# Another weave of the delta rule's streams, and the low parts of the first attention's queries and keys through a diagonal matmul

## The reference

```python
# first attention: 16 heads of width 8 (h=16, d=8), gated weights
qkv = jnp.einsum('bnk,ok->bno', x, g_qkv * qkv_weight)
dots = jnp.einsum('bhid,bhjd->bhij', q, k) * scale
out = jnp.einsum('bhij,bhjd->bhid', jax.nn.softmax(dots, axis=-1), v)
...
# delta rule: 16 heads of width 64, one state W per sequence and head
def step(W, inp):
    q_t, k_t, v_t, b_t = inp
    err = v_t - jnp.einsum('bhij,bhj->bhi', W, k_t)
    W_new = W + b_t[..., None, None] * jnp.einsum('bhi,bhj->bhij', err, k_t)
    return (W_new, jnp.einsum('bhij,bhj->bhi', W_new, q_t))
```

## Time and profile before

| | |
|---|---|
| median of 3 runs | 1710.97 us |
| the profiled execution: its time, its span | 1703.88 us, 1702.1 us |
| busy: PE, DVE, ACT, POOL | 1498.6, 1211.1, 909.4, 694.8 us |
| first attention | about 15 to 250 us of the span |
| the delta rule's 16 units | about 1098 to 1572 us |
| mean granted TensorE clock | 0.961 of full speed |

### The profile page before, as it was taken

One profiled execution on the slowest core, in us unless ns is written; L12 is line 12 of the kernel. 1 busy time (PEld: TensorE's weight loads), 2 busy tenths in 40 slices (PEclk: granted clock), 3 DMA queues, 4 the chain that ended last, 5 costly groups with the idle time before them and its releaser, 6 DMA issues.

```text
span 1702.1 us, 42055 instructions
## 1 busy us (share of the span) xinstructions
PE 1498.6 (88%) x18200; PEld 809.8 (48%) x18200; DVE 1211.1 (71%) x2245; ACT 909.4 (53%) x1269; POOL 694.8 (41%) x732
## 2 busy tenths in 40 slices
PE   7888878999999999999988877889888888989995
PEld 4222223333334334333424544777777777765452
DVE  7788877988857785867527668576777665574866
ACT  1676675777756675786582333545445543342210
POOL 1111131566555564665580107448675556000000
PEclk9898999999999999999999999989999999989898
DMA  4000003332222231432302000000000001100000
GB/s 155 1 1 1 1 1 112 100 88 80 82 72 72 73 102 44 115 85 72 88 1 79 1 1 13 15 15 16 4 16 16 16 4 45 43 3 1 7 7 13
DMA packets 32409, 70.66 MB, mean 42 GB/s; under 512 B 5328, under 2 KB 7056, under 8 KB 31968
## 3 DMA queue, kind: packets, MB, share of 16 engines
q1 hardware_dynamic: 32224, 67.98, 13.6%
HBM read 47.45 MB, written 20.51 MB: 40 GB/s over the span
## 4 chain that ended last, share of the span: by engine, by line
PE 55%; DVE 28%; ACT 8%; issue 6%; POOL 3%; DMA 0%; SPq 0%; ACTq 0%; DVEq 0%; POOLq 0%
PE ps L159 52%; DVE a_MX L408 5%; DVE b_mx L864 2%; ACT b_X L924 1%; POOL d_XI L1744 1%; PE ps L227 1%; POOL d_tmp L1741 1%; DVE st L171 1%; ACT d_L L168 1%; PE ps L1555 1%; DVE b_rd L1034 1%; DVE sq L206 1%; DVE b_VL L799 1%; DVE d_XE L1678 1%; DVE d_KV L1632 1%
## 5 line engine op out<-in xcount | busy, mean ns | idle before, releaser
L942 POOL TENSOR_TENSOR b_EL<-b_X,b_EH 128x1024 f16<-128x1024 f32 x160 | 341.2, 2133 | 235.6 <-ACT b_EH L168 235.6
L924 ACT ACTIVATE b_X<-ps 128x1024 f32<-128x1024 f32 x160 | 163.6, 1022 | 119.0 <-PE ps L159 117.6
L1741 POOL TENSOR_TENSOR d_tmp<-d_G,d_XI 128x31 f32<-128x31 f32 (+15 forms) x248 | 127.8, 515 | 184.3 <-DVE d_G L1670 165.5
L864 DVE TENSOR_REDUCE b_mx<-ps 128x2 f32<-128x1024 f32 x128 | 156.0, 1219 | 50.3 <-PE ps L159 48.6
L168 ACT ACTIVATE b_EH<-b_X 128x1024 f16<-128x1024 f32 x160 | 169.1, 1057 | 34.4 <-PE ps L159 23.2
L159 PE MATMUL ps<-b_M,b_S 128*128 128x512 f16 (+1 forms) x768 | 178.3, 386 | 2.4 <-ACT b_X L924 2.4
L408 DVE TENSOR_REDUCE a_MX<-ps 128x2 f16<-128x1024 f32 x128 | 155.2, 1225 | 27.4 <-PE ps L159 26.1
L445 ACT ACTIVATE a_E<-ps 128x1024 f32<-128x1024 f32 x128 | 131.1, 1024 | 76.1 <-PE ps L159 75.5
L1744 POOL TENSOR_TENSOR d_XI<-d_XI,d_tmp 128x31 f32<-128x31 f32 (+15 forms) x248 | 142.0, 573 | 19.4
L427 POOL TENSOR_TENSOR a_QS<-a_QS,a_MR 128x512 f16<-128x512 f16 x16 | 18.5, 1155 | 215.8 <-ACT a_MR L168 211.8
L159 PEld LDWEIGHTS ps<-b_M,b_S 128*128 128x128 f16 (+1 forms) x768 | 55.5, 98 | 101.4 <-issue 40.8
(11 more groups left out here) (324 smaller groups left out, 3430.9 us busy)
## 6 DMA issues: line engine op xcount, KB each, us to landing
b_S<-s_xk SPq DMA_DIRECT2D x48, 336.0 KB, 6.4
b_M<-s_xq SPq DMA_DIRECT2D x48, 256.0 KB, 5.1
s_xk<-b_Hk SPq DMA_DIRECT2D x16, 336.0 KB, 2.2
s_xk<-b_Lk SPq DMA_DIRECT2D x16, 336.0 KB, 2.4
s_xq<-b_Hq SPq DMA_DIRECT2D x16, 256.0 KB, 2.0
s_xq<-b_Lq SPq DMA_DIRECT2D x16, 256.0 KB, 2.0
d_XI<-eye SPq DMA_DIRECT2D x8, 512.0 KB, 3.7
f_w<-f_w SPq DMA_DIRECT2D x1, 2048.0 KB, 8.5
```

The source lines that it names most:

```text
L864: last = v.e.tensor_reduce(b_mx[:, 0, :, n], PS[:, bk:bk + 2, :], AX, ALU.max)
L924: a.e.activation(b_X[k % 2], PS[:, bk:bk + 2, :], ACT.Exp, scale=0.125).then_inc(sem("b_ex"), 1)
L942: last = p.e.tensor_tensor(b_EL[k % 6], b_X[k % 2], b_EH[k % 6], ALU.subtract)
L1741: e.tensor_tensor(tm, a, x, ALU.mult).then_inc(*p.step())
```

## The change

**First attention.** Two diagonal matrices a_dg (fp16, identity times the constant of queries and of keys) are made once on DVE. The product of a_HI with the constant is no longer made by DVE at the store: PE adds it to AUX with one 128x128x512 fp16 matmul (`a_lower_tensor`, start=False, in slots 1 and 3), and ACT then copies AUX to a_QS or a_KS (`a_store_scalar`, slots 1 and 3). `a_project_vector` is gone. ACT's rounding no longer waits on the store's semaphore, since PE's order covers it.

**Delta rule.** Only the order of instructions changes, by other numbers in the weave and a start value for two streams. The solves and all other matmuls are the same instructions as before. The weight 35 in `c_order` equals the old expression.

```diff
+        a_dg = rA.take("a_dg", 128, F16).rearrange("p (k n) -> p k n", k=2)
...
+            for k in range(2):
+                e.tensor_scalar(a_dg[:, k], ident16[:], a_cst[:, k:k + 1], None, ALU.mult).then_inc(sem("id16"), 1)
...
+        def a_lower_tensor(t, G, k):
+
+            t.wait_ge("id16", 3)
+            t.wait_ge("a_hi", 2 * G + k + 1)
+            mm(t.e, PS[:, AUX, :], a_dg[:, k], a_HI[k], start=False).then_inc(sem("a_qk"), 1)
...
-        def a_project_vector(v, G, k):
-            out = (a_QS, a_KS)[k][G % 4]
-            v.wait_ge("ld_cst", 16)
-            v.wait_ge("a_hi", 2 * G + k + 1)
-            v.wait_ge("a_sc", 8 * (G - 3))
-            stt(v.e, out, a_HI[k], a_cst[:, k:k + 1], PS[:, AUX, :], ALU.mult, ALU.add).then_inc(sem("a_st"), 1)
+        def a_store_scalar(a, G, k):
+            a.wait_ge("a_qk", 4 * G + 2 * k + 2)
+            a.wait_ge("a_sc", 8 * (G - 3))
+            copy(a.e, (a_QS, a_KS)[k][G % 4], PS[:, AUX, :]).then_inc(sem("a_st"), 1)
...
+                    if s in (1, 3) and p + 1 < NG:
+                        a_lower_tensor(t, p + 1, s // 2)
...
+        PREP_LEAD = {"dve": 0.25, "act": -0.25, "pe": 0.25}
+        ROWS_LEAD = {"pe": 0.5, "act": 0.25}
...
-                streams = [(chain(lane, u), 9)]
+                streams = [(chain(lane, u), 8.62)]
...
-                    streams.append((prep(lane, u + 1), 17))
+                    streams.append((prep(lane, u + 1), 17.34, -PREP_LEAD.get(lane.name, 0)))
...
-                    streams.append((rows(lane, m + 1), D_ROWS))
+                    streams.append((rows(lane, m + 1), 18.34, -ROWS_LEAD.get(lane.name, 0)))
...
-                    streams.append((later(13, turn(lane, m)), 30))
-                    streams.append((later(16, blocks(lane, m)), 24))
+                    streams.append((later(18, turn(lane, m)), 30.59))
+                    streams.append((later(22, blocks(lane, m)), 24))
```

More of the change, by code:

```diff
@@ L24 @@
 SHARED = {
-    "e_km": ("a_qk", 32), "e_kp": ("a_hi", 32), "e_vm": ("a_st", 32), "e_vp": ("a_vp", 4), "e_qm": ("a_v", 4),
+    "e_km": ("a_qk", 64), "e_kp": ("a_hi", 32), "e_vm": ("a_st", 32), "e_vp": ("a_vp", 4), "e_qm": ("a_v", 4),
     "e_q": ("a_mt", 128), "e_sm": ("a_mx", 128), "e_ms": ("a_mg", 16), "e_ng": ("a_mrow", 16), "e_mk": ("a_q2", 16),
@@ L35, in weave @@
 def weave(*streams):
-    live = [[g, n, 0] for g, n in streams]
+    live = [[x[0], x[1], x[2] if len(x) > 2 else 0] for x in streams]
     while live:
@@ L264, in build @@
         a_rec = rA.take("a_rec", 32)
+        a_dg = rA.take("a_dg", 128, F16).rearrange("p (k n) -> p k n", k=2)
+        assert rA.word <= 32160, rA.word
         rA = Room(nc, 38944)
@@ L299, in a_load_vector @@
             e.tensor_copy(ident16[:], ident[:]).then_inc(sem("id16"), 1)
+            v.wait_ge("ld_cst", 16)
+            v.wait_ge("id16", 1)
+            for k in range(2):
+                e.tensor_scalar(a_dg[:, k], ident16[:], a_cst[:, k:k + 1], None, ALU.mult).then_inc(sem("id16"), 1)
         def a_load_out_vector(v):
@@ L340, in a_split_gpsimd @@
                 p.wait_ge(f"ld_xt{b}", 16)
-                p.wait_ge("a_qk", 8 * (b - 1) if b > 2 else 0)
+                p.wait_ge("a_qk", 16 * (b - 1) - 1 if b > 2 else 0)
             e.tensor_copy(x[:, 0], w).then_inc(*p.step())
@@ L527, in a_tensor @@
                 hold(t, ACC, (16, 8)[k])
+                a_lower_tensor(t, 0, k)
             keys = b_keys_tensor(t, 0)
@@ L562, in a_scalar @@
                 a_project_scalar(a, 0, k)
+                a_store_scalar(a, 0, k)
             side = a_side(a, a_out_scalar, b_keys_scalar)
@@ L572, in a_scalar @@
                         a_project_scalar(a, p + 1, s // 2)
+                    if s in (1, 3) and p + 1 < NG:
+                        a_store_scalar(a, p + 1, s // 2)
                     if s == 4 and 0 < p <= NG:
@@ L585, in a_vector @@
             keys = b_keys_vector(v, 0)
-            for k in range(2):
-                a_project_vector(v, 0, k)
             side = a_side(v, a_out_vector, b_keys_vector)
@@ L597, in a_vector @@
                         a_den_vector(v, G - 1)
-                    if s in (1, 3) and p + 1 < NG:
-                        a_project_vector(v, p + 1, s // 2)
                     if p in (1, 2):
@@ L1403, in c_order @@
             second = experts(lane, 1)
-            weave((tail, B_OUT + 10), (both(experts(lane, 0, begun), part(second, 4)), 13))
+            weave((tail, 35), (both(experts(lane, 0, begun), part(second, 4)), 13))
             first = both(parts(lane, 0), both(rows(lane, 0), later(7, both(turn(lane, 0), blocks(lane)))))
@@ L2063, in d_order @@
                 m = u // 2 + 2
-                streams = [(chain(lane, u), 9)]
+                streams = [(chain(lane, u), 8.62)]
                 if u == 0:
-                    streams.append((keys(lane, 2), D_KEYS))
+                    streams.append((keys(lane, 2), 26.29))
                 if u == 1:
-                    streams.append((later(1, blocks(lane, 2)), 24))
+                    streams.append((later(0, blocks(lane, 2)), 24))
                 if u % 2 == 0 and u < 14:
-                    streams.append((later(20, back(lane, u // 2 + 1)), 24))
+                    streams.append((later(21, back(lane, u // 2 + 1)), 24))
                 if u + 1 < 16:
-                    streams.append((prep(lane, u + 1), 17))
+                    streams.append((prep(lane, u + 1), 17.34, -PREP_LEAD.get(lane.name, 0)))
                 if u % 2 and m + 1 < NH:
-                    streams.append((rows(lane, m + 1), D_ROWS))
+                    streams.append((rows(lane, m + 1), 18.34, -ROWS_LEAD.get(lane.name, 0)))
                 if u % 2 == 0 and 2 < m < NH:
-                    streams.append((later(13, turn(lane, m)), 30))
-                    streams.append((later(16, blocks(lane, m)), 24))
+                    streams.append((later(18, turn(lane, m)), 30.59))
+                    streams.append((later(22, blocks(lane, m)), 24))
                 if u in (2, 6):
@@ L2080, in d_order @@
                 if u in D_LATE:
-                    streams.append((late(lane, D_LATE[u]), 14))
+                    streams.append((late(lane, D_LATE[u]), 14.48))
                 if u > 12:
```

3 lines of the change are left out of this document (1 added, 2 removed).

## The result

The changed kernel takes 1668.6 us (median of 4 runs) against 1711.22 for the kernel before: ratio 0.9763, 95% interval 0.9729 to 0.9798. A second comparison, with six and seventeen runs, gave 1672.25 against 1707.57, ratio 0.9807 (0.9764 to 0.9849); one of the seventeen, 1909.62 us at a granted clock of 0.734, is left out of that ratio. So it is faster by 33 to 41 us, where I forecast 14.7.

What follows compares the result with a forecast made beforehand. PE, busy 88% of the time, was taken as the bound, so order could win only where it waits. Attention -1.7 and delta rule -13 made -14.7 us, taking the median 1710.97 to 1696; range 1683 to 1711.

Steps and rivals of the forecast that it cites:

- d_AT: Delta rule, two units: PE's wait of 1.75 us for this tile goes to zero, mean gain 1.7 us.
- d_OT: Delta rule, two units: outputs come ahead of the projection, so PE's wait for ACT's copy shrinks; 1.5 us gained.
- the chain: Delta rule: of PE's chain waits, 2.0 us a pair of units, half is taken as gained, -1.0 us.
- The wait for d_KT: Delta rule, two units: a new wait, as the gram matrix needs copies of key turns standing in a row; +0.85 us.
- that for the fold: Delta rule, odd units: a new wait, as the fold comes sooner behind the corner while ACT copies more keys; +0.5 us.
- POOL's wait for d_G: Delta rule: POOL's inverse waits 15.24 us for d_G; 12 or more would be left, so it stays hidden.
- A plain group: First attention, groups without layer norm: plus 0.5 us each (12.94 to 13.47), seven counted, +3.7 us.
- the terms -3.9 and +1.0: First attention: six stores among DVE-bound layer-norm pieces save 0.65 us each; four among small pieces cost 0.25 each.
- its rival's +8: First attention: costs +8 us if all 15 groups pay 0.5 and none gains, total 1706; no chance of its own.
- The rule on the clock: Attention group at 158.81: the page's rule lets shorter waits give back 1.5 us; the forecast said DVE sets the length, nothing gained.
- trade waits: Rival, delta rule: PE leaves one wait and meets the next, giving 0 to -5 us, about 1707; chance 0.20.
- The lump of transposes: Rival, delta rule: four DVE transposes together hold the values' scaling, a pair loses 2.1 us, total 1720; chance 0.10.

Runs made afterwards that it cites:

- mix: The changed kernel with the old weights and no leads in the weaves of units 1 to 11: 1670.1 us, ratio 0.9781.
- attention_only: The kernel before with the first attention's part of the change alone, the delta rule in its old order: 1699.8 us, ratio 0.9953.
- before_plus32: The kernel before with 32 more clock-holding matmuls at the program's start, equal columns: 1705.0 us, ratio 0.9984.
- after_again: The changed kernel, nothing altered, measured a second time against the kernel before: 1672.3 us, ratio 0.9807.
- delta_plus32: The kernel before with the delta rule's new order alone and 32 more clock-holding matmuls at the program's start: 1671.9 us, ratio 0.9790.
- after_less32: The changed kernel with 32 fewer clock-holding matmuls at the program's start, equal columns: 1688.3 us, ratio 0.9891.
- delta_order: The kernel before with the delta rule's new order alone, the first attention as it was: 1691.4 us, ratio 0.9902.
- ends_plus32: The kernel before with 32 more start matmuls and the new weights and leads only in units 0 and 12 to 15: 1702.4 us, ratio 0.9970.
- delta_shifts: The kernel before with only the later turns, blocks and back transposes and the turn's new weight: 1689.4 us, ratio 0.9898.
- the four positions: The changed kernel with 32 fewer, 0, 32 more and 64 more matmuls at the program's start: 1688.3, 1672.3, 1668.7 and 1678.4 us.

## Why the prediction was right or wrong

**The removed waits: right in the main. The bound: not.** Per pair (the list's 280 or 260 us hold 5.2 pairs) d_AT gave 0.8 where I took 1.7 (0.6 us a time are left, where I said none), d_OT 1.1 where I took 1.5, and the chain 1.5 where I took 1.0. The wait for d_KT is 0.9 where it stands (0.85 forecast), that for the fold 1.2 (0.5 forecast). POOL's wait for d_G fell to 11.05 us, so the inverse stays hidden. The pairs took 49.73, 49.82, 49.85, 50.41 and 46.25 us where I said about 50.4 (before: 53.46, 54.73, 52.03, 54.37 and 49.60), and the middle gave 18.1 us instead of 13. I had said that an order can win only where PE waits. Units 1 to 11 before and after:

```profile
1154.07:1418.27 264.20, 234.97 (x6973) 198.41 (x6973) 180.68 (x386) 130.44 (x220) 177.08 (x323) 0.99 0.04 12
...
1143.08:1389.13 246.05, 225.48 (x6975) 196.28 (x6972) 183.13 (x385) 129.88 (x220) 171.82 (x318) 1.00 0.04 12
```

PE's idle time fell by 8.7 us, and its busy time by 9.5 for the same matmuls. mix, with the old weights there and also at a clock of 1.00, has PE busy for 231.58 us, so some 6 of the 9.5 come with the weights; by what, the rows do not show.

**The attention: its sum is neither confirmed nor refuted.** A plain group costs 0.60 more (0.53 forecast), and there are four of them and one at 0.47, not seven. The six groups with layer norm change by -1.3, -1.3, -0.2, +0.1, -1.5 and -0.3, -4.4 in all, where the terms -3.9 and +1.0 made -2.9. Part of that is the clock, which stood at 0.90, 0.90 and 0.78 in the first three of them before; in other traces at full clock the old attention has 16.85, 16.22 and 13.98 us there in place of 16.65, 16.76 and 15.56. Three pairs of kernels at equal position differ by the attention alone: attention_only against before_plus32 (-5.3 us by the ratios), after_again against delta_plus32 (+2.9), after_less32 against delta_order (-1.9). Their mean is -1.4, forecast -1.7, but each is as uncertain as 7 to 10 us; at equal clock they are -0.2, +2.2 and +0.8. So no gain of the attention by itself is shown, and its rival's +8 is out. The first profiles had put 5.5 us on the early passes, but most of that was the clock: in the one trace it was down for 17.1 us ahead of the first reciprocal, in the other for 6.8; after_again, with 17.1 us of it, has that reciprocal at 72.4 beside 73.5 before, not 68.0.

**The rule on the clock: the page was right for this group, and I was not.** In the earlier trace rows I set two different groups side by side. Here is one and the same group, with the same instructions, between the same two reciprocals (a_rec, line 474), in the profile before and in that of before_plus32:

```profile
159.95:175.51 15.56, 13.64 (x78) 2.89 (x78) 13.17 (x26) 10.21 (x12) 1.16 (x1) 0.78 0.00 1
...
163.22:177.19 13.97, 11.24 (x78) 3.01 (x78) 12.84 (x26) 10.12 (x12) 1.15 (x1) 1.00 0.00 0
```

At full clock it takes 1.6 us less; I had said that it gives nothing. In the changed kernel it takes 15.34 at 0.89:

```profile
154.10:169.44 15.34, 12.86 (x80) 3.10 (x80) 12.12 (x24) 11.23 (x14) 1.15 (x1) 0.89 0.00 0
```

and in mix, which has the same attention, 16.40 at 0.79; none of its nine traces has the group at full clock. The old attention has 14.82 at 0.88 (ends_plus32) and 16.01 at 0.79 (delta_shifts), so at like clock the change makes this group 0.4 to 0.5 us longer, not shorter. The Trainium skill's rule (TensorE: Matmul & The Clock Gate, What's actually happening) would have let shorter waits give 1.5 us back. That the clock is worth this much here, the two rows show; that shorter waits raise it, no run here shows.

**The failing steps are two.** The first is "The first two and last four units have other mixes, and I give them 0 (from +3 to -3)": in the traces they gave 4.5 and 9.6 us, 1.1 each of it moved work and part of it clock (unit 0 to 1 ran at 0.88 before and 1.00 after, units 11 to 15 at 0.94 and 0.96). In units 11 to 15 PE's idle time fell by 4.5 us. It comes with the new weights, which I never costed outside of the pair that I had read; its size no timing confirms. The second is a term that the sum lacks. I priced PE's small matmuls at their rate and looked for what they wait for among tiles, banks and copies. Under a denser order PE also waits for its own code, 10 to 24 us of it, and an edit elsewhere moves that: the attention's 32 matmuls, forecast at 0.25 us each and little else, are worth 14 to 19 us to the delta rule. At the code's old position the new order gives 16.7 us, near my 13, but by luck: the middle, where I had all of it, gave 5.1 us there and the first two and last four units, where I had none, 10.8. At the new position the middle gives 19.6 (before_plus32 to delta_plus32), so its term was too small as well. The result is larger because the change carries its own shift, and by the 4 to 12 us that go with a higher clock, for which the sum had no term. Over the four positions the changed kernel's mean is 1677 us.

**The last 6 us.** The first profile of the changed kernel ends 5.9 us sooner behind unit 15. That is chance: the same kernel a second time lacks it, and behind unit 15 all 18 traces take 126.3 or 132.2 us to within 0.1, nine of them each, with either order. Windows of 40 us, of the changed kernel's first execution, where PE stays at full clock:

```profile
1560.00:1600.00 40.00, 37.72 (x200) 19.62 (x199) 30.97 (x94) 8.35 (x16) 1.58 (x1) 1.00 0.02 8
```

and of after_again:

```profile
1560.00:1600.00 40.00, 39.80 (x183) 19.66 (x181) 28.29 (x90) 10.96 (x20) 1.58 (x1) 0.79 0.02 7
```

**The rivals.** The order did more than trade waits, though the mix shows that trade in its pure form. The lump of transposes stood, but did not hold the values: DVE had 1.44 us to spare.
